# A gated recurrent scan with a hyperbolic transformer block: the order of the work past the scan, cut into some 730 pieces with ticks of their own

## The reference, cut to what matters

```python
# x [8, 256, 128], cond [8, 128]; stage 1 on x.reshape(8, 256, 128), 256 steps in turn
def step(h, xt):                              # UGRNN
    m = concat([xt, h]) @ weight + bias
    g, c = sigmoid(m[:, :128] + 1), tanh(m[:, 128:])
    return g * h + (1 - g) * c
x = x + scan(step, cond, x)
# stage 2, per batch, 16 heads of 8; expmap0/logmap0 rescale a row by tanh(n)/n, arctanh(n)/n
ada = cond @ w_ada + b_ada                    # six vectors per batch
u  = expmap0(layer_norm(logmap0(x)) * (1 + sc_msa) + sh_msa)
q, k, v = (to_heads(plin(u, w, b)) for w, b in ...)     # plin: expmap0(logmap0(.) @ w + b)
out_h = expmap0(softmax(qt @ kt.T / sqrt(8)) @ vt)      # 256 x 256 per head, no mask
y  = mobius_add(x, expmap0(g_msa * logmap0(plin(from_heads(out_h), w_o, b_o))))
ff = plin(plin(expmap0(layer_norm(logmap0(y)) * (1 + sc_mlp) + sh_mlp), w_f1, b_f1), w_f2, b_f2)
out = x + mobius_add(y, expmap0(g_mlp * logmap0(ff)))
```

## Time and profile before

| | us |
|---|---|
| median of 3 runs (518.01 to 518.96) | 518.32 |
| the profiled execution's own time | 518.43 |
| its span, first to last instruction | 516.6 |

### The profile page before, as it was taken

How to read it: one execution, slowest core, us unless ns; L and a number is a source line. 1 busy time by engine, 2 the same in 40 slices (tenths; PEclk the granted TensorE clock), 3 DMA queues, 4 the chain that set the end, 5 groups by cost and what they waited for, 6 DMA issues and landing times.

```text
span 516.6 us, 14056 instructions
## 1 busy us (share of the span) xinstructions
PE 371.6 (72%) x5194; PEld 257.1 (50%) x5194; DVE 326.1 (63%) x1939; ACT 217.1 (42%) x963; POOL 141.8 (27%) x295
## 2 busy tenths in 40 slices
PE   2998897968576867699999998585966849354310
PEld 1646665746455655465666565363433626242310
DVE  6444444767775758865757764457037487797874
ACT  2233223234243243355454455445866575631410
POOL 6000000131820233800232710443002152624442
PEclk9999999999999999999999999985798787856555
DMA  7109200200000000000000000000000000000000
GB/s 170 46 4 191 57 1 1 44 1 3 2 3 1 2 1 3 2 1 3 1 4 1 2 3 2 3 2 0 3 1 1 2 1 3 20 2 21 1 20 21
DMA packets 9114, 8.42 MB, mean 16 GB/s; under 512 B 1275, under 2 KB 7693, under 8 KB 9046
## 3 DMA queue, kind: packets, MB, share of 16 engines
q1 hardware_dynamic: 8950, 7.26, 6.3%
q0 software_dynamic: 96, 0.26, 0.2%
HBM read 6.45 MB, written 1.08 MB: 15 GB/s over the span
## 4 chain that ended last, share of the span: by engine, by line
PE 50%; DVE 28%; ACT 10%; issue 5%; POOL 4%; DMA 1%; SPq 0%; DVEq 0%; POOLq 0%; ACTq 0%
PE zb L750 18%; PE tb L855 5%; PE tb L701 5%; DVE prod_hi L1356 4%; ACT state L1110 3%; PE firsts L898 3%; PE zb L729 3%; PE firsts L987 3%; DVE prod_lo L1362 2%; PE firsts L919 2%; ACT state L1113 2%; PE zb L735 2%; PE zb L966 1%; PE firsts L750 1%; POOL stat L651 1%
## 5 line engine op out<-in xcount | busy, mean ns | idle before, releaser
L750 PEld LDWEIGHTS zb<-prod_hi,whh 128*128 128x128 f16 x1920 | 73.5, 106 | 96.1 <-DVE prod_hi L1356 88.6
L750 PE MATMUL zb<-prod_hi,whh 128*128 128x8 f16 x1920 | 90.7, 171 | 41.6 <-DVE prod_hi L1356 40.5
L1110 ACT ACTIVATE state<-zb 128x8 f32<-128x8 f32 x240 | 42.6, 177 | 169.4 <-PE zb L750 169.4
L1356 DVE SCALAR_TENSOR_TENSOR prod_hi<-state 128x16 f16<-128x16 f32 x255 | 47.5, 186 | 98.9 <-ACT state L1113 95.1
L750 PE MATMUL zb<-prod_lo,whh 128*128 128x8 f16 x960 | 63.6, 172 | 2.6 <-DVE prod_lo L1362 0.8
L1362 DVE TENSOR_TENSOR prod_lo<-prod,prod_hi 128x16 f16<-128x16 f32 x255 | 50.7, 199 | 8.7
L750 PEld LDWEIGHTS zb<-prod_lo,whh 128*128 128x128 f16 x960 | 44.4, 107 | 6.2 <-DVE prod_lo L1362 2.9
L1244 ACT ACTIVATE prd<-zb 128x640 f32<-128x640 f32 x64 | 41.6, 703 | 12.7 <-PE zb L966 12.3
L560 POOL TENSOR_TENSOR stat<-mv 128x4 f32<-128x4 f32 x4 | 0.8, 206 | 159.4 <-DVE mv L1450 159.4
L1358 DVE SCALAR_TENSOR_TENSOR prod<-state 128x16 f32<-128x16 f32 x256 | 43.4, 169 | 0.5 <-ACT state L1113 0.5
L1113 ACT ACTIVATE state<-zb 128x16 f32<-128x16 f32 x240 | 42.7, 178 | 0.0
(11 more groups left out here) (324 smaller groups left out, 745.3 us busy)
## 6 DMA issues: line engine op xcount, KB each, us to landing
mod<-ada_rows SPq DMA_DIRECT2D x4, 768.0 KB, 12.2
resid<-in_x_dram SPq DMA_DIRECT2D x6, 128.0 KB, 3.7
ffz<-shift_rows SPq DMA_DIRECT2D x4, 131.0 KB, 3.3
out_dram<-state SPq DMA_DIRECT2D x8, 64.0 KB, 2.1
out_dram<-early SPq DMA_DIRECT2D x8, 64.0 KB, 2.1
yy<-in_L_cond_w_ada_dram SPq DMA_DIRECT2D x1, 384.0 KB
early<-in_L_cond_weight_dram SPq DMA_DIRECT2D x2, 128.0 KB
resid<-in_x_dram POOLq DMA_DIRECT2D x2, 128.0 KB, 3.5
```

The source lines that it names most:

```text
L750: i = pe.matmul(z_bank(t, k)[:, NB * (t % CH):NB * (t % CH) + NB], whh[:, half, p, k, :], src[:, NB * p:NB * p + NB], start=False, stop=Fa ...
L1110: act.activation(r[:, 24:32], z_bank(t, 1)[:, k:k + NB], ACT.Tanh, scale=-1.0 / ZS)
L1356: dve.scalar_tensor_tensor(prod_hi[:, :], r[:, 16:32], 1.0, r[:, 0:16], ALU.add, ALU.mult).then_inc(hi_ready, 1)
```

## The change

It replaces the tick tables for the work past the scan and cuts that work more finely. Before, a worker stopped at some 20 to 60 places there; now at some 730 over all engines, and each has its own tick in `TOK_LAST`, `TAIL0` to `TAIL3` and `DIAG`. The ticks no longer stand for scan steps: they run from 0 to about 1600, counted from the scan's end, and are sorted by when the inputs of a piece are there and by the longest chain that is left behind it. The scan's own part, ticks and chunks 0 to 2, keeps its order. Own-result waits on DVE are moved from behind the producer to in front of the consumer, for the count that the consumer needs (`settle(mark)`), with a stopping place between the two, so that pieces of other workers can stand there. No instruction that computes is added or taken away; the DMAs stay as they are, behind the same semaphores.

```diff
-LAST = STEPS + 66
-TAIL = dict(
-    ot=(0, 2), o=(1, 3), oT=5, oevac=3, wo=8, m=14, wosq=15, asq=11, adot=16, norm=20, tanh=26,
...
-PLAN = dict(
-    tails=(49, 89, 141, 180), gaps=(5, 5, 5, 5, 5, 5, 5, 5))
+TAIL3 = dict(
+    ot=(1096, 1104), o=(1107, 1128), oT=1138, oevac=1158, wo=1164, m=1188, wosq=1203, asq=1216,
...
+DIAG = dict(
+    scores=(364, 368, 379, 384, 391, 407, 409, 426, 428, 441, 447, 457, 458, 473, 475, 485, 491,
...
+        def part(now, base, T, name, k=None):
+            if T is TOK:
+                yield
+            else:
+                yield from at_ticks(now, base + (T[name + "_"] if k is None else T[name + "_"][k]))
...
-            def settle():
-                dve.wait_ge(dve_done, done[0])
+            def settle(n=None):
+                dve.wait_ge(dve_done, done[0] if n is None else n)
...
                 for op_, waits in chain:
                     done_(op_())
                     if waits:
-                        settle()
+                        mark = done[0]
+                        if T is not TOK or n % 3 == 2:
+                            yield from part(now, base, T, "artanh", n)
+                        settle(mark)
                         n += 1
-                        if n % per_piece == 0:
-                            yield
...
-                settle()
-                settled(dve.tensor_scalar(xy, xy, 2.0, 1.0, ALU.mult, ALU.add))
+                mark = done[0]
+                yield from part(now, base, T, name, 1)
+                settle(mark)
+                done_(dve.tensor_scalar(xy, xy, 2.0, 1.0, ALU.mult, ALU.add))
+                mark = done[0]
+                yield from part(now, base, T, name, 2)
+                settle(mark)
...
-                for g in range(NG):
-                    yield from at_ticks(now, diag_tick(g))
-                    scores(g, 0)
+                for g in range(NG + 2):
+                    if g < NG:
+                        yield from at_ticks(now, STEPS + DIAG["scores"][2 * g])
+                        scores(g, 0)
                     if g >= 2:
+                        yield from at_ticks(now, STEPS + DIAG["values"][g - 2])
                         values(g - 2)
```

More of the change, by code:

```diff
@@ L141 @@
-TURN = {(j, u): n for n, (_, j, u) in enumerate(USES)}
+USES = [(j, PSUM_USERS[k]) for _, j, k in sorted((t, j, k) for j in range(NJ)
+                                                for k, (_, t) in enumerate(psum_ticks(j)))]
+TURN = {use: n for n, use in enumerate(USES)}
+END = STEPS + max(max(t["out"], t["add"]) for t in TAILS) + 60
 def att_groups():
@@ L615, in tokens @@
                                        ALU.add).then_inc(tok_u, 1)
-                    yield from at_ticks(now, base + TOK["clip"])
+                    yield from at_ticks(now, base + T["clip"])
                     pool.wait_ge(tok_usq, c + 1)
@@ L619, in tokens @@
                     for q in range(2):
-                        yield from at_ticks(now, base + TOK["factor"][q])
+                        yield from at_ticks(now, base + T["factor"][q])
                         if (c, q) != (NC - 1, 1):
@@ L625, in tokens @@
                     for q in range(2):
-                        yield from at_ticks(now, base + TOK["values"][q])
+                        yield from at_ticks(now, base + T["values"][q])
                         pool.wait_ge(factors, 2 * c + q + 1)
@@ L843, in tokens @@
                         if j == 3:
-                            yield
+                            yield from part(now, base, T, "utrans")
                             pe.wait_ge(tok_u, c + 1)
@@ L849, in tokens @@
                         for n in range(2):
-                            yield from at_ticks(now, base + TOK["qkv"] + 2 * j + n)
+                            yield from at_ticks(now, base + T["qkv"][2 * j + n])
                             if n == 0:
@@ L859, in tokens @@
                     for j in range(NJ):
-                        yield from at_ticks(now, base + TOK["stack"][j])
+                        yield from at_ticks(now, base + T["stack"][j])
                         n = NJ * c + j
@@ L874, in tokens @@
                             if k == 0:
-                                yield
+                                yield from part(now, base, T, "stack", j)
                         i.then_inc(stack_ps, 1)
@@ L926, in attention @@
                 for g in range(len(GROUPS)):
-                    yield from at_ticks(now, GROUPS[g][6])
+                    yield from at_ticks(now, GROUPS[g][6] if g < EARLY else STEPS + DIAG["before"][g - EARLY])
                     scores(g)
@@ L1165, in tokens @@
                                         [SW, CH]), ACT.Copy).then_inc(h_copied, 1)
[L1166 removed]
+                    yield from at_ticks(now, base + T["xna"])
                     act.wait_ge(tok_rho, c + 1)
@@ L1194, in tokens @@
                         n = NJ * c + j
-                        yield from at_ticks(now, base + TOK["qsq"] + 2 * j)
+                        yield from at_ticks(now, base + T["qsq"][j])
                         act.wait_ge(qkv_copied, n + 1)
@@ L1380, in prepare, with artanh @@
                 yield
-            def artanh(k, sel, tag, var, wait, ready, per_piece):
+            def artanh(now, base, T, k, sel, tag, var, wait, ready):
                 c = st("cl" + tag, sel)
@@ L1465, in tokens @@
                         n = NJ * c + j
-                        yield from at_ticks(now, base + TOK["yevac"] + 2 * j)
+                        yield from at_ticks(now, base + T["yevac"][j])
                         dve.wait_ge(qkv_ps, n + 1)
@@ L1537, in head_sums @@
                     return
-                yield
+                yield from part(now, tok_base(c), tok_ticks(c), "qreduce", q)
                 dve.wait_ge(qkv_reduced, n + 1)
@@ L1567, in attention @@
                     g = NI * b + NI - 1
-                    yield from at_ticks(now, diag_tick(g + 2) + (1 if b < NB - 1 else 0))
+                    yield from at_ticks(now, STEPS + DIAG["saved"][b])
                     dve.wait_ge(diag_pv, g + 1)
@@ L1583, in mobius @@
                 done_(dve.tensor_scalar(w, x2s, -1.0, 1.0, ALU.mult, ALU.add))
-                settle()
+                mark = done[0]
+                yield from part(now, base, T, name, 0)
+                settle(mark)
                 done_(dve.tensor_tensor(xy, dots, tau, ALU.mult))
@@ L1659, in work @@
                     dve.wait_ge(att_th, j + 1)
-                    mobius(j, sel, "a", st("adot", sel), st("ss1", sel)).then_inc(att_co, 1)
+                    last = yield from mobius(now, base, T, "mob", j, sel, "a", st("adot", sel), st("ss1", sel))
+                    last.then_inc(att_co, 1)
+                    yield from part(now, base, T, "ss", 0)
                     pp, qq, mm = st("aP", sel), st("aQ", sel), st_of("asq", 1, sel)
@@ L1670, in work @@
                     done_(dve.tensor_tensor(var, qq, st("msum", sel), ALU.mult))
-                    settle()
+                    mark = done[0]
+                    yield from part(now, base, T, "ss", 1)
+                    settle(mark)
                     done_(dve.scalar_tensor_tensor(e1, e2, 2.0, e1, ALU.mult, ALU.add))
@@ L1764, in work @@
                     ins.then_inc(f2_y, 1)
+                    yield from at_ticks(now, base + T["ffm"])
                     dve.wait_ge(f2_y, j + 1)
@@ L1785, in work @@
                                                                ALU.mult, ALU.add))
-                            settle()
+                            mark = done[0]
+                            yield from part(now, base, T, "out", q)
+                            settle(mark)
                             for c in (q, q + 2):
```

296 lines of the change are left out of this document (197 added, 99 removed), and 3 rows, old and new, of the table scores.

## The result

| | before | changed |
|---|---|---|
| median, us | 518.16 (4 runs, 513.73 to 518.96) | 487.22 (4 runs, 486.36 to 487.79) |
| profiled execution, span, us | 518.43, 516.6 | 487.77, 485.5 |
| DVE, whole span | 326.1 us, 63% | 318.4 us, 66% |

Ratio of the medians 0.9418, 95% interval 0.9362 to 0.9474: faster by 5.8%. The forecast of 490.9 us lies 3.7 us above the median, inside its range; "faster" had 0.90.

The account below looks back on a forecast made before the run. Past the scan, chains through in-order engines set the end, ready links standing behind waiting ones. Scan 315.7, then 38.0 + 77 + 54.8 + 3.6, gave 489.1 us span, plus 1.8 makes 490.9; own range 481 to 499, wider bounds 481 to 506.

Parts of the forecast that it names:

- the opened waits: Small DVE instructions: 0.11 us open per own-result wait, 52 waits after the last sum into O, three fifths filled, 3.4 us.
- C: From the last sum into O's end to the last DVE instruction: 63.6 us becomes 54.8, bounds 50 and 62.
- B: From the first diagonal scores to the last sum into O's end: 89.4 us becomes 77, bounds 70 and 88.
- A: From the scan's end to the first diagonal scores: 44.3 us becomes 38.0, bounds 36 and 42.
- The rival that the waits fill nothing: Later DVE instructions can't use the 0.11 us gaps past the scan; total 495 us, chance 0.06.
- I cost that at nothing: Arctanh waits moved behind scan steps in chunks 0 to 2: no effect, 2 us at worst either way.
- The early start of the units: Diagonal units start behind stacking of tiles 0 and 1 only: of 8.8 us, 5.1 stay and 3.7 go.
- The collision of an addition with tail 3's arctanh: After the last sum into O, a 128x512 POOL addition holds a small DVE instruction once more, costing 1.1 us.
- the 11.7 us off tail 3's chain: After the last sum into O: 7.7 us from earlier transposes on PE plus 4.0 from the root on POOL.
- The clock rival: TensorE stays at 1.2 GHz in the diagonal stage, which stays at 89 us or so; total 503, chance 0.09.
- The slower one: Tails' steps stall in-order PE between diagonal units; 1.7 us at each of 22 steps loses the gain; chance 0.06.
- the last one: Nothing moves where it counts: the tick tables yield nearly the old order at the hand-overs; chance 0.03.

Follow-up runs that it names:

- e1: Changed kernel with the same order, but each DVE own-result wait put back right behind its producer, scan part too; 498.52 us.
- e6: Changed kernel with all four tiles' stacking transposes put back ahead of the first diagonal unit; 490.97 us.
- e2: Changed kernel with coarse DVE pieces past the scan: first pieces keep their ticks, later ones follow at once; 502.26 us.
- e3: Changed kernel with POOL's addition for tail 2 moved behind tail 3's inverse root; 486.05 us.
- e4: Changed kernel with the last sum into O moved ahead of tail 2's Möbius coefficients and tail 1's output on DVE; 486.08 us.
- e7: Changed kernel with 68 idle products on PE in the holes after the last sum into O, to keep its clock up; 487.81 us.
- e11: Changed kernel with both the last sum into O earlier and tail 2's POOL addition behind tail 3's root; 485.97 us.
- e12: Changed kernel with coarse DVE pieces past the scan and own-result waits back behind their producers; 504.22 us.
- e9: Kernel before, order kept, with own-result waits of the arctanh chains alone moved behind existing stopping places; 513.02 us.

## Why the prediction was right, and where it was wrong

**The total was right with two errors of opposite sign.** It had the new order at 27.5 - 4.4 = 23.1 us and the opened waits at 4.4 (3.4 in C, 1 in B). e1 gives 19.7 to the order (518.16 to 498.52) and 11.3 to the waits.

**The opened waits** are the term that was sized too low. The step "52 x 0.11 = 5.7 us, of which three fifths" had the right mechanism and the right price of one gap, but counted only C, and there two arctanh chains and two sets of Möbius coefficients. The waits are open in all of B, in the norms, sums and reciprocals too, and in the scan. e1 against the changed kernel, by the two traces, which lie 12.6 us apart and not 11.3: scan 1.5, A -0.3, B 5.3, C 6.1 us. The rival that the waits fill nothing had 495 us; without them it is 498.5. The count had to come from every place where `settle(mark)` stands behind a stopping place. The order, in turn, was sized too high, most of all in B: without the opened waits the prediction has B at 78, and in e1 it was 82.9. That the two errors cancel is luck.

**Scan.** "I cost that at nothing", with 2 us as the bound: some 1.1 us are gained by step 160 (medians 196.5 and 197.6 us of the two sets of traces).

**A, 38.0 forecast, 36.3 measured.** The early start of the units was sized well: 8.8 us became 4.9 and not 5.1, and e6 takes 3.4 us of A back. The start of the head scaling moved 4.1 us and not the 2.6 of the two waits for the copies. The other 1.5 I can't assign to one step; it isn't the waits (e1's A is 36.0), but it is in part the piece sizes (e2's A is 38.9).

**B, 77 forecast, 77.6 measured.** PE's busy time was 63.2 us and not 67.4, but at a density of 0.81 and not 0.84; the two misses cancel for the most part. The clock rose to 0.85, as supposed. The waits of units for exponentials and tails went, as the prediction said from the earlier trace rows, and a new wait of 4.0 us for the last sum into O came in, which it did not foresee. By e1, 5.3 us of B's gain come from the opened waits, where the prediction had 1.

**C, 54.8 forecast, 53.3 measured.** Waits for other engines fell by 5.0 us (6.5 forecast); the overlap did more (C is 6.1 us shorter than e1's, some 0.6 of it by the clock, against 3.4 forecast). The DVE's whole idle time in C is 6.6 us, not below the 5 that was named as a sign of being right; 5.0 of it are waits for other engines. The collision of an addition with tail 3's arctanh came as sized, 1.1 us:

```profile
463.51 1.26 POOL L717 TENSOR_TENSOR early<-early,resid 128x512 f32<-128x512 f32 x1 [3.88 <-DVE early L1888]
463.55 1.25 DVE L1459 SCALAR_TENSOR_TENSOR stat<-tmp 128x4 f32<-128x4 f32 x1
...
464.87 1.03 POOL L701 TENSOR_TENSOR stat<-stat,neg_half 128x4 f32<-128x4 f32 x1
```

The choice to size C by the DVE's idle time and not by the 11.7 us off tail 3's chain is borne out by the experiments, not by the number: the chain alone gives 63.6 - 11.7 + 1.1 = 53.0, as near to 53.3 (from the end of the last sum into O to the root it went from 46.6 us to 36.3, 10.3). But in e3, e4, e7 and e11, each of which shortens a link of that chain, the median moved by 1.3 us at most, and in e1, with the same order, C is 59.4.

**The rivals.** The clock rival did not come (0.85 in B). The slower one did not: the worst wait of PE for a tail's step in B was 2.7 us, beside the 4.0 for the last sum into O, where it needed 1.7 at each of 22 steps. The order moved, so the last one is out too.

**What stays open.** Which of the order's 19.7 us belongs to which move: only the start of the units (3.75 by the medians, 1.9 to 3.3 by the traces, e6) and the places of the DVE pieces (3.8 past the scan, e12 against e1) were taken apart. Whether opened waits need the new order to be worth something is open too: e9 opened too few of them. Whether e4 or e11 beats the changed kernel is at the edge of what these runs tell.

## What to carry to other kernels

Put an own-result wait in front of the instruction that needs it, with another chain's work between, and count every such place, not only those in the last chain: here all of them together were worth 11.3 us in the new order, and 30 of them in the old order 0.7 us past the scan. Where an in-order engine is 94% full up to the last hand-over, as here, a single link moved ahead was given back for the most part by the work that it passed; look at covered time in the stretch before moving one. A coarse order lost twice here, by the places and by the gaps that nobody fills.

## What the runs showed of the hardware

- Own-result waits cost the DVE covered time: 125.8 us with them behind the producer, 117.6 in front of the consumer, for the same instructions in the same order.
- An addition of 128x512 on POOL often held a DVE instruction of [128 x 4] until it had ended: 1.27 us before, 1.25 in the changed kernel, 1.22 in e11, 0.71 for a product with a scalar at 428.45. The Trainium skill, SBUF — State Buffer, section SBUF: two separate sides, calls the shared port pair an exclusive lock held for the whole instruction, and these rows agree. Not every instruction is held: in e2 the addition at 478.70 stood beside DVE instructions with an input in PSUM (`early<-tb,xT`), which took their usual 0.28 us.
- The scan's time did not depend on TensorE's clock here. In e4's profiled execution the granted clock was at its lower level from about 85 us on, through the rest of the scan, as this slice row of its page shows (tenths, 40 slices), and the scan ended at 313.8 us, the earliest but two:

```profile
PEclk9999998555555555555555555555679989755565
```
